# First pair's statistics, transposes and maximum moved forward; fourth projection unit moved ahead of the reciprocal spread, in a fused group-norm, attention and displacement kernel

## What is computed

```python
# layer 0: group norm (32 groups), attention of 12 heads over N = 1024 positions, projection, residual
qkv = x_flat @ W_qkv.T                       # only k and v are needed
var_v = jnp.var(v, axis=-1, ddof=1, keepdims=True)
var_k = jnp.var(k, axis=-1, ddof=1, keepdims=True)
scores = var_v @ jnp.swapaxes(var_k, -2, -1) * scale
out = jax.nn.softmax(scores, axis=-1) @ v
out = out @ W_proj.T + b_proj                # x = x + out
# layer 1: group norm, each channel shifted by a whole offset and masked,
# then a separable 3x3 filter per channel; x = x + result
```

## Time and profile before

| | us |
|---|---|
| median of 3 runs | 2196.28 |
| lowest and highest run | 2188.87, 2200.17 |
| the profiled execution, device time | 2193.13 |
| its span, first to last instruction | 2191.6 |
| TensorE busy (matmul) | 2019.3, 92% |
| VectorE busy | 1704.5, 78% |
| ScalarE busy | 1186.4, 54% |
| mean granted TensorE clock | 0.975 |

### The profile page before, as it was taken

One profiled execution on the slowest core, in us unless ns is written; L12 is line 12 of the kernel. 1 busy time (PEld: TensorE's weight loads), 2 busy tenths in 40 slices (PEclk: granted clock), 3 DMA queues, 4 the chain that ended last, 5 costly groups with the idle time before them and its releaser, 6 DMA issues.

```text
span 2191.6 us, 36482 instructions
## 1 busy us (share of the span) xinstructions
PE 2019.3 (92%) x13100; PEld 1112.6 (51%) x13100; DVE 1704.5 (78%) x3695; ACT 1186.4 (54%) x1285; POOL 184.2 (8%) x215
## 2 busy tenths in 40 slices
PE   3899999999999999999999999999999999999970
PEld 2656356653656436563365535655365543665330
DVE  7587667987689875998769986798759987699738
ACT  5376634665266742667336762566437674267601
POOL 2000000100001100110001100011001010011001
PEclk8999999999999999999999999999999999999985
DMA  6411302334033521335013350234312251133304
GB/s 235 149 50 59 97 1 80 128 111 140 11 107 117 153 72 40 108 114 171 26 50 126 119 164 2 97 117 125 119 40 103 102 168 45 40 127 117 117 1 173
DMA packets 103021, 214.81 MB, mean 98 GB/s; under 512 B 50080, under 2 KB 50848, under 8 KB 102816
## 3 DMA queue, kind: packets, MB, share of 16 engines
q1 hardware_dynamic: 70848, 95.79, 14.5%
q0 software_dynamic: 25920, 94.38, 11.6%
q10 hardware_dynamic: 6048, 22.02, 3.1%
HBM read 154.08 MB, written 57.74 MB: 97 GB/s over the span
## 4 chain that ended last, share of the span: by engine, by line
PE 69%; DMA 12%; DVE 11%; issue 4%; ACT 2%; SPq 1%; POOL 1%; ACTq 0%; DVEq 0%; POOLq 0%
PE ps L1117 28%; PE ps L1156 21%; PE ps L1173 15%; DMA a_sb<-a_rows 4%; PE ps L1138 3%; DVE st L762 2%; ACT ring L606 2%; DVE bst_x L736 2%; DMA a_rows<-at 2%; DMA cs_rows_y<-mv_y 1%; DMA r_rows<-dt_sb 1%; DMA bt<-r_rows 1%; DMA dt_sb<-d_sb 1%; DVE d_sb L823 1%; DVE bt L813 1%
## 5 line engine op out<-in xcount | busy, mean ns | idle before, releaser
L606 ACT ACTIVATE ring<-a_sb,coef 128x1024 f32<-128x1024 f32 x768 | 814.1, 1136 | 57.9 <-DMA a_sb<-a_rows 41.7
L1117 PE MATMUL ps<-wkv_hi,h_sp 128*128 128x256 f16 x4608 | 785.6, 275 | 13.5 <-DVE h_sp L753 10.2
L1156 PE MATMUL ps<-ring,xv 128*64 128x512 f32 x3072 | 694.7, 597 | 9.3 <-ACT ring L606 6.3
L1117 PE MATMUL ps<-wkv_lo,h_sp 128*128 128x256 f16 x2304 | 634.1, 275 | 0.0
L1117 PEld LDWEIGHTS ps<-wkv_hi,h_sp 128*128 128x128 f16 x4608 | 454.9, 99 | 104.2 <-issue 30.6
L813 DVE TENSOR_TENSOR bt<-bt,ring 128x1024 f32<-128x1024 f32 x416 | 484.9, 1214 | 1.9 <-ACT ring L606 1.8
L1156 PEld LDWEIGHTS ps<-ring,xv 128*64 128x64 f32 x3072 | 206.1, 136 | 423.0 <-issue 374.0
L590 ACT ACTIVATE xv<-ps 128x256 f32<-128x256 f32 x192 | 73.8, 384 | 579.6 <-DVE st L762 579.6
L1173 PE MATMUL ps<-xv,wp_hi 128*128 128x512 f16 x1152 | 350.5, 382 | 9.7 <-issue 9.7
L762 DVE BATCH_NORM_STATS2 st<-ps 128x6 f32<-128x64 f32 x1536 | 218.5, 216 | 81.8 <-PE ps L1117 80.7
L1117 PEld LDWEIGHTS ps<-wkv_lo,h_sp 128*128 128x128 f16 x2304 | 227.4, 99 | 28.0
(11 more groups left out here) (127 smaller groups left out, 1341.7 us busy)
## 6 DMA issues: line engine op xcount, KB each, us to landing
a_sb<-a_rows SPq DMA_DIRECT2D x96, 512.0 KB, 4.7
xv<-in_x POOLq DMA_DIRECT2D x48, 512.0 KB, 3.7
h_sp<-in_x ACTq DMA_DIRECT2D x42, 512.0 KB, 4.8
shift_rows<-bt POOLq DMA_DIRECT2D x42, 512.0 KB, 3.0
out<-xv POOLq DMA_DIRECT2D x42, 512.0 KB, 2.9
bt<-r_rows SPq DMA_DIRECT2D x80, 256.0 KB, 3.9
shift_rows<-ring SPq DMA_DIRECT2D x12, 528.0 KB, 14.1
xv<-in_L_conv_W_qkv SPq DMA_DIRECT2D x4, 1152.0 KB, 9.0
```

The costliest lines, as they stand in the source:

```text
L606: nc.scalar.activation(ring_of(p, s, m), a_sb[:, h % 4, :], ACT.Exp, scale=coef[:, h, m:m + 1]).then_inc(s_exp, 1)
L1117: last = nc.tensor.matmul(ps[:, kv_bank[u % 2], half * 2 * P:(half + 1) * 2 * P], h_sp[:, k, hp, m * P:(m + 1) * P], wkv[wpart][:, k, q * ...
L1156: last = nc.tensor.matmul(ps[s * HD:(s + 1) * HD, o_bank[p % 2] + j, :], v_sb[:, p, m, s * HD:(s + 1) * HD], ring_of(p, s, m)[:, j * HALF: ...
```

## The change

No instruction is added or dropped; the order changes on TensorE and VectorE.

- In stage one, unit 4 is issued in halves: first half, the transposes of pair 0, second half, the spread of pair 0. The spread stood behind unit 5, the transposes behind unit 4. Unit 4's semaphore increment comes with its second half.
- On VectorE `k_max` of pair 0 follows `variances` directly, ahead of `masks_y`, `gn` and unit 4's statistics; `k_scales` follows unit 4's statistics instead of unit 5's. In the first pass the evictions of the projection weights (`beside`) now stand ahead of `variances`.
- In the span, pair 0 alone: the statistics of units 6 and 7 and `variances` of pair 1 stand ahead of step 0 instead of behind the additions of step 3.
- In the projection, unit 3's matmuls for k = 2 and 3 stand ahead of `r_spread` instead of behind it.

```diff
@@ DVE, phase_a @@
+                    if beside is not None:
+                        beside(u)
                     if u == UQ - 1:
                         variances(b, 0)
+                        k_max(b, 0, l1 is not None)
                         if l1 is not None:
                             masks_y(l1)
                             gn(l1, 0, g_t)
-                    if beside is not None:
-                        beside(u)
                     if u == UQ:
-                        k_max(b, 0, l1 is not None)
-                    if u == UQ + 1:
                         k_scales(b, 0)
@@ DVE, span @@
                     nxt = UA + p * UQ
+                    if p == 0:
+                        kv_stats(b, nxt)
+                        kv_stats(b, nxt + 1)
+                        variances(b, 1)
                     for m in range(MT):
                         add_up(b, p, m, later)
                         if m == 3:
-                            if p <= 4:
+                            if 1 <= p <= 4:
                                 kv_stats(b, nxt)
...
@@ PE, kv_unit @@
-            def kv_unit(b, u, later):
+            def kv_unit(b, u, later, halves=(0, 1)):
...
-                if u >= 2:
+                if halves[0] == 1:
+                    pass
+                elif u >= 2:
                     pe.wait_ge(s_bn, b * NU + u - 1)
                     pe.wait_ge(s_vev, b * NU + u - 1)
...
-                for half in (0, 1):
+                for half in halves:
...
-                last.then_inc(s_kv, 1)
+                if halves[-1] == 1:
+                    last.then_inc(s_kv, 1)
@@ PE, phase_a @@
-                    kv_unit(b, u, later)
+                    if u == UQ:
+                        kv_unit(b, u, later, (0,))
+                        k_transpose(b, 0)
+                        kv_unit(b, u, later, (1,))
+                        k_spread(b, 0)
+                    else:
+                        kv_unit(b, u, later)
                     if beside is not None:
                         beside(u)
-                    if u == UQ:
-                        k_transpose(b, 0)
-                    if u == UQ + 1:
-                        k_spread(b, 0)
@@ PE, phase_c @@
                 project(b, 2, range(CT - 2))
-                project(b, 3, range(2))
+                project(b, 3, range(CT - 2))
                 r_spread(b)
-                project(b, 3, range(2, CT - 2))
```

## The result

The changed kernel takes 2157.53 us (median of 4 runs, 2156.49 to 2161.23), the kernel before beside it on the same chip 2192.57 us (4 runs, 2188.54 to 2200.17). The ratio is 0.984, with an interval of 0.981 to 0.987: faster, by 35 us. The profiled executions have spans of 2154.9 and 2191.6 us, 36.7 us apart. Lines of kernel.py have moved by 3 to 8: the key and value matmuls are L1122 (before L1117), the transposes L1132 and L1133, the spread L1137, the denominators L1144, the weighings L1162, the projection L1179, its evictions L973.

The account below looks back on a forecast made before the run. TensorE, holding 69% of the chain, was taken as the bound through its waits and half clock; 33.5 - 0.5 + 3.5 = 36.5 us gave 2156.6 to 2159.8, forecast 2158 us, range 2146 to 2176.

Parts of the forecast that it names:

- The stretch: Unit 3 to weighing 4 in seven later passes: 37.1 us each instead of 293.19 in all, gaining 33.5 us.
- The wait amid unit 4: TensorE at pair 0's transposes between unit 4's halves: a new wait of 0.45 us for VectorE's maxima.
- The wait at the spread: TensorE at pair 1's spread, ahead of weighing 4: a new wait of 0.6 us for VectorE's diagonal.
- The diagonal: VectorE's input to pair 1's spread: done at 1145.65, after units 8 and 9 end at 1145.05.
- The exponentials: ScalarE, first pair: transposes read 2.2 us earlier, row write, broadcasts and exponentials moving with it by the same 2.2 us.
- rival 1: Broadcasts of the attention rows land no earlier, meeting the normalised rows' write and gather: 7 us lost, 2165 us; chance 0.11.
- The half clock behind the maxima: Units 8 and 9 behind pair 1's transposes: 7.27 us of half clock in seven passes goes with the idling.
- The projection: Fourth unit ahead of the spread of reciprocals: 3.5 us gained, range 3.1 to 6.5, seventh unit waiting about 0.8 us.
- VectorE catching up: Behind the stretch: VectorE, 3.4 us further behind TensorE, catches up within two or three pairs, costed at nothing.
- The first pass: No idling to remove there; the half-unit wait costs about 0.5 us, the later additions fit by 1.6 us.
- Rivals 2 to 5: Half clock stays or moves, 0.11; VectorE becomes the bound, 0.07; rival 4, 0.03; pair 4 or 5 returns the gain, 0.06.
- rival 4: Additions behind unit 7's statistics end too late; VectorE 6 us slower to the diagonal cancels a pass's gain; chance 0.03.

Follow-up runs that it names:

- the projection alone: Kernel before with only the fourth projection unit's matmuls moved ahead of the spread of reciprocals: 2191.42 us, ratio 0.998.
- the version with both waits removed: Changed kernel with projection unit 0 evicted before the group statistics are spread and pair 1's maximum read ahead of the taps: 2150.98 us, again 2148.42 us.
- the maximum alone: Kernel before with only pair 0's transposes amid unit 4 and its maximum ahead of the masks: 2158.65 us, ratio 0.984.
- the early eviction: Changed kernel with VectorE evicting projection unit 0 before the next image's group statistics are spread: 2157.39 us, ratio 0.981.

## Why the prediction was right, point by point

It said 2158 us and 36.5 us less; the spans differ by 36.7, the medians by 35, and the median is 2157.53. That the spans come within 0.2 us is partly luck: 0.55 us more in the stretches and 0.85 more around the projection are set off by 1.3 us more lost in the first pass, where two profiles of one program differ by more. Of its steps:

- **The stretch**: 37.1 us forecast, 37.02 in every pass; 33.5 us forecast for the seven, 34.05 measured. This carried the result.
- **The wait amid unit 4**: 0.45 forecast, 0.34 to 0.35. **The wait at the spread**: 0.6 forecast, 0.49 to 0.50. **The diagonal**, forecast to be done 36.74 us behind unit 3's start (1145.65), is done at 36.59 (1129.24 + 0.21).
- **The exponentials**: this term was mis-sized. I let them keep their distance from the read of the transposes and got 2.2 us; the second head's gained 4.7. The 2.2 is there (the transposes are read 6.91 us behind unit 3's start, 9.13 before); the row write adds 1.76, and from the broadcasts' issue to the second head's exponential it is 6.7 us instead of 7.46. The experiments put 0.8 us of the row write on the tile write ahead of it, and a comparison of passes puts 1.0 us on an instruction packet amid it. With the row landed early the broadcasts are issued 8.92 us behind unit 3's start, ahead of the tile write at 9.71; the prediction had them at 10.7, behind it. I had looked at that queue for the opposite sign only (rival 1). The wrong size did no harm to the sum, because weighings 1 to 4 run unhindered with either.
- **The half clock behind the maxima**: gone from units 8 and 9 in all seven passes, as the sum had it. It goes with the wait of 2.98 us: it is there in the run of the projection alone and in the one that only delays the tile write, and absent where the wait is 0.34 to 1.47.
- **The projection**: 3.5 forecast, about 4.35. The seventh unit waits 0.39 to 0.78 us, 0.8 forecast. The half clock left one of the two passes in which it stood and stayed in the other, behind 2.22 us: I had taken it to stay in both. The new spell of half clock, at the start of one pass's projection, was not in the sum.
- **VectorE catching up**: nothing grew behind the stretch (105.89 us both).
- **The first pass**: 0.5 us loss forecast; a wait of 0.30 us or none is there, and the rest can't be resolved.

What the prediction did not see is how little of the change was needed. It took the moved statistics to be what removes the 2.99 us wait. The run without them shows that wait gone as well: with exponentials 4.7 us early the additions end in time in their old place. The argument was right in its sum with a redundant part in it.

Rival 1 (broadcasts no earlier) took the wrong sign, though a late second broadcast, its mechanism, does occur: once in seven passes, 1.28 us, hidden. The rule that transfers from several queues interleave on the same engines holds as the trace shows it (Trainium skill, "Trainium Kernel Development and Optimization", section Key Constraints): a tile write issued 0.8 us behind the broadcasts takes 6.6 us to land here, 3.4 before, when it went first. It names no loser; in both kernels the transfer issued later was the one held up, but for the pass with the late broadcast, in which both were slow (7.67 us and 7.47 for the tile write). Rivals 2 to 5 did not come: no half clock in the stretches (one spell of it is new in a projection), TensorE kept its 5.9 us in the pass that I walked through (42.92 less 37.02), no pass came near rival 4's point, and pair 4 and 5 returned nothing.

## What to carry to other kernels

Where two queues send at the same time, look at which transfer is issued first: a small write on the critical path right behind a large one of another queue pays for it, and reordering the compute can shift that by accident, for or against. If two edits of a change remove the same wait, their gains do not add; a run with each alone tells which is needed. The instruction packets that the profile lists among the DMA queues are worth a look too: one amid a small write went with 1.0 us more. And a wait that a new order makes (0.34, 0.50, 0.7 us here) is worth a second look at once: moving one eviction and one small reduction took away another 8.2 us of waits, and 10.6 us of the median.

## What the runs showed of the hardware

- An 8 KB write (16 packets of 512 bytes on SyncE's queue) issued 1.08 us behind a 512 KB write on GpSimd's landed 3.09 to 3.24 us after its issue in six passes and 2.12 in the seventh; with the large write held back, 2.31 to 2.57 and 1.34; with the large write behind it, in the changed kernel, 1.34 in all seven. The passes with the 1.0 us more are those in which an 8192-byte instruction packet starts before the row's last packet.
- The second of two 512 KB broadcasts made ScalarE wait 0.5 to 1.7 us in nine of 49 passes (two profiles each of the changed kernel and of the version with both waits removed, and those of the maximum alone, without the statistics, and with the early eviction), though the issues before it stand alike. What makes it late is open.
- TensorE's granted clock stayed at 1.00 (2.4 GHz) behind waits of 0.34 to 1.47 us for the maxima of either pair. Behind waits of 2.98 us for the second pair's, units 8 and 9 ran partly at half clock (1.2 GHz) in 13 of 20 passes (the kernel before, the projection alone, the tile write later), and behind the one of 2.26 us. Behind the waits for the reciprocals in all fourteen profiles, half clock followed on none of the 15 under 0.99 us (from 0.25 up), on 9 of the 17 from 0.99 to 1.69, and on 11 of the 13 from 2.01 to 3.63. TensorE often idles at the start of the projection too, some 7 us ahead of these, so that a single wait need not be the whole of it.
